# Expert block of a routed layer: the twelve gate and up products in one piece, the next block's token transposes after them

## Chip, cores, metric

One NeuronCore of a Trainium2 chip runs one program. The metric is the device time of one execution in microseconds (us); the median of three runs is given. Engines are named as in the profile: PE is TensorE's matmul, PEld its weight load, DVE is VectorE, ACT is ScalarE, POOL is GpSimd, SP is SyncE. A suffix q (PEldq, DVEq) marks an instruction that the engine's sequencer handles alone, such as register arithmetic, a branch or a wait.

## What is computed

Two transformer-like layers over 2048 tokens of 512 numbers. The first has linear attention and an int8 feed-forward part, the second a gated cumulative attention and a routed part with 32 experts, of which each token uses 8. The change touches only the routed part. Cut to it, the reference is:

```
router_probs = softmax(x @ gate_weight.T); top 8 of 32 experts, some rerouted -> combine[token, expert]
for each expert e:
    gu = x @ wgu[e].T                      # 512 -> 384
    g, u = split(gu, 2)                    # 192 each
    h = silu(g) * u
    y = y + h @ wd[e].T * combine[:, e]    # 192 -> 512
```

## The kernel before

The first 1000 us or so compute the two attention parts, the int8 part and the routing tables. The routed part then works on 159 blocks (NBLK) of 128 rows. A block holds tokens of one expert; on average an expert has five blocks. Each number of the token rows and of h is carried as two float16 numbers, a high half and a low half, and each expert weight too, so a float32 product becomes three float16 products: high by high, high by low, low by high.

What one block k passes through:

- POOL gathers its 128 token rows by an indirect DMA (L1712) into one of eight buffers. It does so eight blocks ahead. Rows of a block are in `xg`, which the trace shows as XT.
- PE transposes them, eight transposes of 128x128 (`gather_transposes`, L816). DVE copies the result out of PSUM in one instruction (L1268) and raises the semaphore `xt_sb`.
- PE computes gate and up together: twelve products of 384 columns (`gate_up`, L825). The list `products` holds the pairs (0,0), (0,1), (1,0) of token half and weight half, four parts of the 512 inputs each. The last one raises `gu_ready`.
- ACT takes silu of the gate half (L1548). DVE multiplies it with the up half and the combine weight (L1278) and raises `h_ready`. ACT writes the high half of h (L1306), DVE the low half in two instructions (L1280, L1281), which raises `h_lo`.
- PE transposes h, three transposes (`h_transposes`, L835). ACT copies them out (L1306), and PE runs five products of 512 columns (`expert_down`, L846) with the down weights.
- ACT scales the result out of PSUM (L1306, X<-bank), and POOL adds it to DRAM by an indirect DMA (L1718). There are two accumulators; a scatter waits for the one two blocks before it.

Each engine has its own instruction stream, written out by hand. PE's iteration for block k is: down products of block k-3, gate and up products of block k with the token transposes of block k+1 in between, h transposes of block k-1. The order on DVE is: copy of the token transposes of block k+1 (it waits for `xt_ready`, L1267 and L1268), h of block k, low half of h of block k. The order on ACT is: silu of block k, copy of the h transposes of block k-1, high half of h of block k, result of block k-2.

The blocks run in a hardware loop unrolled by eight (`every_block`). At the first block of each eight ("fresh") PE and DVE read the packed expert numbers of the next blocks into registers (`load_packs`, L337: one TENSOR_LOAD and some register operations). On PE the loop's branch (L328) and this load stand ahead of the down products of block k-3. The weights of the current expert sit in one of four SBUF slots, so the addresses of the expert's weights are computed by register operations: one (L825, shown by the listing of instructions as ISA) ahead of each of the first eight gate and up products, none ahead of the last four, which reuse the first four's addresses, and four ahead of the five down products.

Waits in PE's iteration: L839 (`ht_sb` of block k-3), L841 (`y_sb`), L859 (weights of the expert), L860 (`xt_sb` of block k; the trace shows it served by the first L825 register operation), L862 (`h_ready`), L811 (the gathered rows of block k+1), L813 (`xt_sb`), L830 (`h_lo` of block k-1), L832 (`ht_sb`).

Of the kernel before, what the change touches and what calls it, by code (L numbers as in the profile page):

```python
# [81 lines left out]
def build(nc, ins, out):  # L82
    ctx = ExitStack()
    with ctx:
# [3 lines left out]
        def sem(name):  # L88
            return ctx.enter_context(nc.semaphore(name))
# [81 lines left out]
        def wc(a, k, c0, n):  # L171
# [107 lines left out]
        xt_ready, xt_sb, gu_ready, sg_ready, h_ready, h_hi, h_lo, ht_ready, ht_sb, blk_done, y_sb = (sem(n) for n in (  # L279
            "xt_ready", "xt_sb", "gu_ready", "sg_ready", "h_ready", "h_hi", "h_lo", "ht_ready", "ht_sb", "blk_done", "y_sb"))  # L280
# [53 lines left out]
        def load_packs(engine, k):  # L334

            at = k.key[0] * 2
            _, words = nc.values_load_multi_w_load_instructions(packs[0:1, bass.ds(at, 3)], (engine,), min_val=0, max_val=(1 << 20) - 1)  # L337
            return words

        def expert_of(words, u):  # L340
            w, shift = words[(u + 4) // 4], (u + 4) % 4
            return (w // (1 << (5 * shift)) if shift else w) % EXPERTS
# [165 lines left out]
        def _(pe):  # L508
# [301 lines left out]
            def gather_transposes(k):  # L810
                pe.wait_ge(xg_in[k.u % NG], k.use(NG) * 16 + 16)  # L811
                if not k.before(2):
                    pe.wait_ge(xt_sb, k.i - 1)  # L813
                d = bank[k.u % 2][:, :].bitcast(F16)
                for c in range(2 * KD):
                    mm = pe.transpose(d[:, c * P:(c + 1) * P], xg[k.u % NG].bitcast(F16)[:, c * P:(c + 1) * P], ident16[:, :])  # L816
                mm.then_inc(xt_ready, 1)

            def weights(sl, j, c0, n):
                return Wslot[:, bass.ds(sl * (2 * WCOLS) + (j * WCOLS + c0), n)]  # L820

            def gate_up(k, sl, some):
                d = bank[2 + k.u % 2][:, 0:2 * DFF]
                for a, b, kd in some:
                    mm = pe.matmul(d, xTb[k.u % 2][:, a * KD + kd, :], weights(sl, b, kd * 2 * DFF, 2 * DFF),  # L825
                                   start=(a, b, kd) == (0, 0, 0), stop=(a, b, kd) == (1, 0, KD - 1))
                return mm

            def h_transposes(k):
                pe.wait_ge(h_lo, k.i + 1)  # L830
                if not k.before(2):
                    pe.wait_ge(ht_sb, k.i - 1)  # L832
                d = bank[4 + k.u % 2][:, :].bitcast(F16)
                for c in range(3):
                    mm = pe.transpose(d[:, c * P:(c + 1) * P], hB[k.u % 2][:, c * P:(c + 1) * P], ident16[:, :])  # L835
                mm.then_inc(ht_ready, 1)

            def expert_down(k, sl):
                pe.wait_ge(ht_sb, k.i + 1)  # L839
                if not k.before(2):  # L840
                    pe.wait_ge(y_sb, k.i - 1)  # L841
                d = bank[6 + k.u % 2][:, :]
                base = KD * 2 * DFF
                order = ((1, 0, base), (1, 1, base), (0, 0, base), (2, 0, base + DIM), (2, 1, base + DIM))
                for n, (c, j, c0) in enumerate(order):
                    mm = pe.matmul(d, hT[k.u % 2][:, c, :], weights(sl, j, c0, DIM), start=n == 0, stop=n == 4)  # L846
                mm.then_inc(blk_done, 1)

            products = [(a, b, kd) for a, b in ((0, 0), (0, 1), (1, 0)) for kd in range(KD)]
            held = {}  # L850

            def expert_block(k, fresh, last=False):
                if fresh:
                    held["packs"] = load_packs(pe.engine, k)
                e = expert_of(held["packs"], k.u)
                if not k.before(3):
                    expert_down(k.at(-3), expert_of(held["packs"], k.u - 3) % NSLOT)
                sl = e % NSLOT
                pe.wait_ge(w_in, e * 16 + 16)  # L859
                pe.wait_ge(xt_sb, k.i + 1)  # L860
                if not k.before(2):
                    pe.wait_ge(h_ready, k.i - 1)  # L862
                gate_up(k, sl, products[:8])
                if not last:
                    gather_transposes(k.at(1))
                gate_up(k, sl, products[8:]).then_inc(gu_ready, 1)
                if not k.before(1):
                    h_transposes(k.at(-1))

            pe.wait_ge(tables_ready, 1)  # L870
            gather_transposes(Blk(0, 0, 8))
            every_block(pe, 8, expert_block, 8)
            final = [Blk(0, NBLK - j, 8) for j in (3, 2, 1)]
            expert_down(final[0], expert_of(held["packs"], NBLK % 8 - 3) % NSLOT)
# [926 lines left out]
```

## Time and profile before

| | us |
|---|---|
| median of 3 runs | 1685.71 |
| lowest, highest | 1683.06, 1691.47 |
| the profiled execution | 1696.52 |
| span in its trace | 1694.7 |
| PE busy in it | 1484.5 (88%) |
| mean granted TensorE clock | 0.945 |

The profiled execution is 10.8 us above the median and 1.8 us longer than its span. Times in the trace are microseconds from the start of the span. A matmul row's own duration includes a modelled end, so how long a group of matmuls holds PE is read from the distance between the starts of groups.

### The profile page before, as it was taken

How to read it: one execution, taken by the hardware profiler on the slowest of the kernel's cores; microseconds unless marked ns; L12 is line 12 of the kernel's file. 1: busy time of each engine (PE TensorE's matmuls, PEld its weight loads, DVE VectorE, ACT ScalarE, POOL GpSimd, SP SyncE). 2: the span in 40 equal slices, each digit the busy share in tenths (PEclk: the TensorE clock that was granted, in tenths of full speed). 3: DMA queues.
4: the chain of work that ended last, by engine and by line, in shares of the span. 5: the costliest groups of instructions: out<-in, count | busy, mean ns of one | idle time of the engine just before them, and what ended most of it. 6: DMA issues, size and time to landing. Idle time of an engine off the chain costs nothing.

```text
span 1694.7 us, 33958 instructions
## 1 busy us (share of the span) xinstructions
PE 1484.5 (88%) x11445; PEld 840.2 (50%) x11446; DVE 974.0 (57%) x1884; ACT 714.9 (42%) x1294; POOL 774.0 (46%) x683
## 2 busy tenths in 40 slices
PE   2699999979999999999996369989988999999980
PEld 1466666644444444445553226545555565665650
DVE  8577777767766666633889664333333343434437
ACT  5233433345454545443555324333433444444430
POOL 3444544451020202044465345565565776666654
PEclk9799999989999999999998569999999999999995
DMA  6331111139786767531111057999999887787868
GB/s 219 113 130 25 25 37 25 25 114 312 258 270 220 264 231 256 183 121 51 52 50 51 3 179 190 249 255 249 263 248 249 161 158 141 143 146 138 147 103 303
DMA packets 96809, 269.44 MB, mean 159 GB/s; under 512 B 15121, under 2 KB 15537, under 8 KB 91889
## 3 DMA queue, kind: packets, MB, share of 16 engines
q1 hardware_dynamic: 61136, 182.75, 32.1%
q0 software_dynamic: 35616, 85.99, 25.9%
q8 instruction: 30, 0.49, 0.1%
q14 instruction: 27, 0.21, 0.0%
HBM read 158.84 MB, written 101.47 MB: 154 GB/s over the span
## 4 chain that ended last, share of the span: by engine, by line
PE 59%; DMA 14%; DVE 14%; issue 6%; ACT 3%; POOL 3%; DVEq 0%; SPq 0%; ACTq 0%; POOLq 0%
PE bank L514 15%; DMA acc<-X,WA 12%; PE bank L825 11%; PE bank L846 6%; PE bank L637 6%; PE bank L643 6%; PE bank L666 6%; PE bank L816 3%; DVE ARENA L1016 2%; ACT ARENA L1306 2%; DMA ARENA<-acc 1%; PE bank L746 1%; DVE ARENA L1194 1%; PE bank L835 1%; PE bank L543 1%
## 5 line engine op out<-in xcount | busy, mean ns | idle before, releaser
L825 PE MATMUL bank<-ARENA,XT 128*128 x1908 | 366.9, 329 | 1.9 <-DVE XT L1268 1.9
L1718 POOL DMA_INDIRECT acc<-X,WA x159 | 252.9, 1590 | 187.1 <-ACT X L1306 143.9
L825 PEld LDWEIGHTS bank<-ARENA,XT 128*128 128x128 f16 x1908 | 181.7, 99 | 125.4 <-issue 10.7
L846 PE MATMUL bank<-ARENA,XT 128*128 x795 | 200.6, 384 | 26.1 <-issue 15.2
L1268 DVE COPY XT<-bank 128x1024 f16<-128x1024 f16 x159 | 109.7, 690 | 189.6 <-PE bank L816 140.3
L1306 ACT ACTIVATE ARENA<-ARENA 128x512 f16<-128x512 f32 (+1 forms) x128 | 92.7, 735 | 263.9 <-DVE ARENA L1044 134.4
L1712 POOL DMA_INDIRECT XT<-x_rows,WA x159 | 157.0, 987 | 56.6 <-issue 35.3
L514 PE MATMUL bank<-WA,XT 128*128 128x512 f16 (+1 forms) x768 | 138.1, 334 | 24.3 <-DVE WA L885 23.5
L1571 POOL TENSOR_TENSOR rstd<-mv,mhalf 128x1 f32<-128x1 f32 x44 | 19.2, 436 | 295.3 <-DVE mv L891 295.3
L514 PE MATMUL bank<-XT,STG 128*128 128x512 f16 x640 | 150.2, 382 | 0.0
L1278 DVE SCALAR_TENSOR_TENSOR XT<-bank,XT 128x192 f32<-128x192 f32 x159 | 66.4, 418 | 140.6 <-ACT XT L1548 117.2
L1548 ACT ACTIVATE XT<-bank 128x192 f32<-128x192 f32 x159 | 52.3, 329 | 212.8 <-PE bank L825 195.1
L1306 ACT ACTIVATE X<-bank 128x512 f32<-128x512 f32 x159 | 93.7, 589 | 114.0 <-DMA acc<-X,WA 86.0
L1306 ACT ACTIVATE XT<-bank 128x384 f16<-128x384 f16 (+2 forms) x207 | 126.0, 609 | 23.9 <-PE bank L503 22.2
L637 PE MATMUL bank<-XT,WA 128*128 (+1 forms) x512 | 122.6, 383 | 8.5 <-issue 8.5
L666 PE MATMUL bank<-ARENA 128*128 128x512 f16 x512 | 121.1, 379 | 3.5 <-DVE ARENA L1050 3.4
L643 PE MATMUL bank<-XT,ARENA 128*128 (+1 forms) x512 | 121.6, 381 | 0.0
L846 PEld LDWEIGHTS bank<-ARENA,XT 128*128 128x128 f16 x795 | 72.8, 98 | 85.8 <-issue 31.0
L1580 POOL TENSOR_TENSOR ARENA<-X,ARENA 128x512 f16<-128x512 f16 (+1 forms) x48 | 68.4, 1436 | 93.1 <-ACT ARENA L1306 93.1
L816 PE MATMUL bank<-ident,XT 128*128 128x128 f16 x1272 | 98.7, 221 | 12.7 <-DMA XT<-x_rows,WA 12.7
L514 PEld LDWEIGHTS bank<-WA,XT 128*128 (+1 forms) x768 | 60.7, 99 | 90.0 <-DVE WA L885 23.1
L816 PEld LDWEIGHTS bank<-ident,XT 128*128 128x128 f16 x1272 | 84.9, 99 | 36.5 <-DMA XT<-x_rows,WA 11.9
(216 smaller groups left out, 2406.7 us busy)
## 6 DMA issues: line engine op xcount, KB each, us to landing
w_scratch<-WA SPq DMA_DIRECT2D x64, 640.0 KB, 3.9
ARENA<-w_scratch SPq DMA_DIRECT2D x32, 1280.0 KB
ARENA<-w_exp SPq DMA_DIRECT2D x48, 640.0 KB, 5.2
WA<-w_exp SPq DMA_DIRECT2D x16, 640.0 KB, 5.0
ARENA<-ARENA SPq DMA_DIRECT2D x64, 128.0 KB, 2.3
acc<-ARENA SPq DMA_DIRECT2D x18, 256.0 KB, 3.0
x_rows<-ARENA SPq DMA_DIRECT2D x17, 256.0 KB, 2.0
STG<-xT SPq DMA_DIRECT2D x8, 512.0 KB, 4.2
```

The source lines that it names most:

```text
L514: mm = pe.matmul(dst, wa(a, k), wb(b, k), start=n == 0, stop=n == 3 * KD - 1)
L637: mm = pe.matmul(bank[0][:, :], Wg[:, n % KD, m * P:(m + 1) * P], XT[:, n // KD, n % KD, tk], start=n == 0, stop=n == 2 * KD - 1)
L643: mm = pe.matmul(bank[1 + m % 2][:, :], Wu[:, n % KD, m * P:(m + 1) * P], XT[:, n // KD, n % KD, tk], start=n == 0, stop=n == 2 * KD - 1)
L666: mm = pe.matmul(bank[4 + tt][:, :], fB[:, m % 2, a, tt * P:(tt + 1) * P], Wd[:, m, :], start=m == 0 and a == 0, stop=m == NM - 1 and a == 1)
L816: mm = pe.transpose(d[:, c * P:(c + 1) * P], xg[k.u % NG].bitcast(F16)[:, c * P:(c + 1) * P], ident16[:, :])
L825: mm = pe.matmul(d, xTb[k.u % 2][:, a * KD + kd, :], weights(sl, b, kd * 2 * DFF, 2 * DFF), start=(a, b, kd) == (0, 0, 0), stop=(a, b, kd) ...
L846: mm = pe.matmul(d, hT[k.u % 2][:, c, :], weights(sl, j, c0, DIM), start=n == 0, stop=n == 4)
L1268: dve.tensor_copy(xTb[k.u % 2].rearrange("p c n -> p (c n)"), bank[k.u % 2][:, :].bitcast(F16)).then_inc(xt_sb, 1)
L1306: return act.activation(dst, src, ACT.Copy, scale=scale)
L1580: pool.tensor_tensor(hl[:, 1, :], tile(t), hl[:, 0, :], ALU.subtract).then_inc(x_lo, 1)
L1712: pool.indirect_dma_start(xg[i % NG], None, xrows, bass.IndirectOffsetOnAxis(blkidx[:, i:i + 1], 0)).then_inc(xg_in[i % NG], 16)
L1718: pool.indirect_dma_start(acc[i % 2], bass.IndirectOffsetOnAxis(blkidx[:, i:i + 1], 0), yD[i % 4], None, compute_op=ALU.add).then_inc(y_ou ...
```

## The change

In PE's iteration the token transposes of block k+1 move from behind the eighth product to behind the twelfth. The signal `gu_ready` stays on the twelfth product. Nothing else moves, and no other engine's order changes.

```
                 if not k.before(2):
                     pe.wait_ge(h_ready, k.i - 1)
-                gate_up(k, sl, products[:8])
+                gate_up(k, sl, products).then_inc(gu_ready, 1)
                 if not last:
                     gather_transposes(k.at(1))
-                gate_up(k, sl, products[8:]).then_inc(gu_ready, 1)
                 if not k.before(1):
                     h_transposes(k.at(-1))
```

On PE, a block in the middle of the unrolled eight. L816 are the token transposes, L825 the gate and up products, L835 the h transposes, and the ISA row of L846 opens the next iteration's down products:

```order
 L825 MATMUL bank3<-ARENA,XT 128x384
 L825 ISA
-L825 MATMUL bank3<-ARENA,XT 128x384
+L825 MATMUL bank3<-ARENA,XT 128x384 x5
 L816 MATMUL bank0<-ident16,XT 128x128 x8
-L825 MATMUL bank3<-ARENA,XT 128x384 x4
 L835 MATMUL bank4<-ident16,XT 128x128 x3
 L846 ISA
```

The four products without register operations now stand behind the eighth one, and eleven transposes follow each other.

On PE, the last block of the unrolled eight, where the loop's branch follows:

```order
 L825 MATMUL bank3<-ARENA,XT 128x384
 L825 ISA
-L825 MATMUL bank3<-ARENA,XT 128x384
+L825 MATMUL bank3<-ARENA,XT 128x384 x5
 L811 ISA
 L816 MATMUL bank0<-ident16,XT 128x128 x8
-L825 MATMUL bank3<-ARENA,XT 128x384 x4
 L835 MATMUL bank4<-ident16,XT 128x128 x3
 L328 REGISTER_ALU
```

The same move; the wait for the gathered rows (L811) moves with the transposes, and the branch still comes right behind the h transposes.

## Rows read from the trace of the kernel before

**Rows 1.** Busy time by stretch of the routed part: us, busy time by engine, PEclk, DMA share.

```profile
core 0: us, PE busy (x) PEld busy (x) DVE busy (x) ACT busy (x) POOL busy (x), PEclk, DMA share, GB/s
1038.00:1095.00 57.00, 54.86 (x422) 34.08 (x420) 22.34 (x58) 23.00 (x58) 31.44 (x25) 1.00 0.89 237
1095.00:1324.00 229.00, 201.78 (x1451) 119.61 (x1449) 78.82 (x211) 84.27 (x209) 135.34 (x105) 0.96 0.93 249
1324.00:1640.00 316.00, 306.84 (x2349) 191.57 (x2348) 128.64 (x334) 133.48 (x335) 217.66 (x169) 1.00 0.81 145
```

**Rows 2.** Timeline, a middle block: start, us, engine line, xcount [idle before it].

```profile
1453.15 0.61 PE L816 MATMUL bank<-ident,XT 128*128 128x128 f16 x8
1453.60 0.81 PE L825 MATMUL bank<-ARENA,XT 128*128 x4
1453.80 0.69 DVE L1268 COPY XT<-bank 128x1024 f16<-128x1024 f16 x1 [1.19 <-issue]
1454.24 0.33 PE L835 MATMUL bank<-ident,XT 128*128 128x128 f16 x3
1454.41 1.24 PE L846 MATMUL bank<-ARENA,XT 128*128 x5
1454.44 0.33 ACT L1548 ACTIVATE XT<-bank 128x192 f32<-128x192 f32 x1 [1.80 <-PE bank L825]
1454.98 0.42 DVE L1278 SCALAR_TENSOR_TENSOR XT<-bank,XT 128x192 f32<-128x192 f32 x1 [0.49 <-ACT XT L1548]
1455.28 1.29 PEld L825 LDWEIGHTS bank<-ARENA,XT 128*128 128x128 f16 x8
1455.49 1.46 PE L825 MATMUL bank<-ARENA,XT 128*128 x8
1456.79 0.61 PE L816 MATMUL bank<-ident,XT 128*128 128x128 f16 x8
```

**Rows 3.** Timeline at the routed part's start, a product that waited for the copy.

```profile
1017.14 0.68 DVE L1268 COPY XT<-bank 128x1024 f16<-128x1024 f16 x1
1018.01 0.42 DVE L1278 SCALAR_TENSOR_TENSOR XT<-bank,XT 128x192 f32<-128x192 f32 x1 [0.19 <-issue]
1018.07 0.23 PEld L825 LDWEIGHTS bank<-ARENA,XT 128*128 128x128 f16 x2 [0.62 <-issue]
1018.07 0.50 PE L825 MATMUL bank<-ARENA,XT 128*128 x2 [0.45 <-DVE XT L1268]
```

**Rows 4.** PE's sequencer around a loop branch, by line (ns, first and last start).

```profile
L825 PEldq FUSED_REGOPS  x8: 46/46/96, 1461.8 to 1462.8; - x8
...
L832 PEldq EVENT_SEMAPHORE  x1: 51/51/51, 1463.2 to 1463.2; - x1
...
L328 PEldq ALU_OP  x1: 32/32/32, 1463.6 to 1463.6; - x1
...
L337 PEldq TENSOR_LOAD <-WA x1: 769/769/769, 1464.1 to 1464.1; - x1
```

**Rows 5.** Timeline from the block before the branch to the second one behind it.

```profile
1461.08 0.69 DVE L1268 COPY XT<-bank 128x1024 f16<-128x1024 f16 x1 [1.13 <-PE bank L816]
...
1462.32 0.42 DVE L1278 SCALAR_TENSOR_TENSOR XT<-bank,XT 128x192 f32<-128x192 f32 x1 [0.55 <-ACT XT L1548]
...
1462.78 1.46 PE L825 MATMUL bank<-ARENA,XT 128*128 x8
...
1463.38 0.22 DVE L1281 TENSOR_TENSOR XT<-XT 128x64 f16<-128x64 f32 x1
...
1466.40 0.77 PEld L846 LDWEIGHTS bank<-ARENA,XT 128*128 128x128 f16 x5 [1.07 <-issue]
1466.43 1.24 PE L846 MATMUL bank<-ARENA,XT 128*128 x5 [0.92 <-ACT XT L1306]
...
1471.15 1.46 PE L825 MATMUL bank<-ARENA,XT 128*128 x8
...
1472.54 0.22 DVE L1281 TENSOR_TENSOR XT<-XT 128x64 f16<-128x64 f32 x1
```

**Rows 6.** Register loads on PE's sequencer, from 1324 us to 1640 us.

```profile
L337 PEldq TENSOR_LOAD <-WA x10: 769/770/1072, 1342.9 to 1615.0; - x10
```

**Rows 7.** Idle time before token transposes and before h transposes, 1040 us to 1324 us.

```profile
  DMA XT<-x_rows,WA: 19.6, 21
...
  DVE XT L1281: 13.9, 24
```

**Rows 8.** Who waited for whom, 1040 us to 1300 us: us, times, longest.

```profile
ACT X L1306 <- DMA acc<-X,WA: 77.7, 21, 6.0
```

More of the change, by code:

```diff
@@ L862, in expert_block @@
                     pe.wait_ge(h_ready, k.i - 1)
-                gate_up(k, sl, products[:8])
+                gate_up(k, sl, products).then_inc(gu_ready, 1)
                 if not last:
                     gather_transposes(k.at(1))
-                gate_up(k, sl, products[8:]).then_inc(gu_ready, 1)
                 if not k.before(1):
```

## The prediction

> **What bounds the kernel now.** I read the busy time by stretch first, since the edit touches only the routed part. From 1324 to 1640 us PE is busy 306.8 of 316 us at full granted clock, so PE sets the pace there, and 84 blocks run. From 1095 to 1324 us PE is busy 201.8 of 229 us, with the DMA engines at 0.93, and blocks come less often. From 1038 to 1095 us PE is busy 54.9 of 57 us [rows 1].
>
> Then the timeline of one middle block. From the start of one group to the start of the next, PE spends 1.30 us on the first eight products (1455.49 to 1456.79), 0.45 on eight token transposes (1453.15 to 1453.60), 0.64 on the last four products, 0.17 on three h transposes and 1.08 on five down products (1454.41 to 1455.49). The sum is 3.64 us, which is also the distance between two blocks (1453.15 to 1456.79): PE never stops in a middle block [rows 2]. There are ten groups of eight in this stretch, since PE's sequencer loads its registers ten times [rows 6]. At such a load PE does stop: the first down product behind it starts at 1466.43, where without a stop it would have started at 1462.78 + 1.30 + 0.45 + 0.64 + 0.17 = 1465.34, by the group lengths above [rows 2, 5]. That is 1.09 us per eight blocks. Check: 84 x 3.64 + 10 x 1.09 = 316.7, the length of the stretch is 316.
>
> Why it stops matters most here. The sequencer rows tell: it takes the first products' register operation at 1461.8, when the DVE copy of the token transposes ends (1461.08 + 0.69 = 1461.77), reaches the waits of the h transposes (L832) at 1463.2 and gets to the loop's branch (L328) at 1463.6, when the low half of h is written (1463.38 + 0.22 = 1463.60). The register load starts at 1464.1 and the first down product's weights at 1466.40 [rows 4, 5]. So branch, load and register work take 2.8 us, and PE is covered only by what the sequencer had queued before it. How early the sequencer gets to the branch is worth PE time, one for one.
>
> **The change part by part.** I use as zero of a block the start of its first product (t0).
>
> *PE's work.* The same 28 matmuls in another order. In each block two changes of kind (product to transpose and back) become one. Eight products take 1.30 us, 0.163 each, four take 0.64, 0.161 each [rows 2], so a change of kind shows no cost to two digits. Term: 0.
>
> *The copy of the token transposes, in middle blocks.* Transposes now start at t0 + 1.30 + 0.64 = 1.94 instead of 1.30. The copy starts 0.65 after them (1453.15 to 1453.80) and takes 0.69 [rows 2], so it ends at t0 + 3.28, and the next block's products are due at 3.64. Before, the copy had 1.00 us to spare, now 0.36. A product that really waited for the copy started 0.25 after its end (1017.14 + 0.68 = 1017.82 to 1018.07), weights and matmul together [rows 3]. So 0.36 - 0.25 = 0.11 us remain and PE does not stop. Term: 0. The weight load of such a first product now starts 0.21 ahead of its matmul (1455.28, 1455.49) [rows 2], and that lead shrinks to 0.11 or less; whether it is needed is a rival below.
>
> *h, in middle blocks.* The copy is ahead of h in DVE's order. Today h waits for silu and starts at 1454.98, which is 3.13 after its block's t0 (1455.49 - 3.64 = 1451.85); now silu comes early (1.94 + 0.20 + 0.33 = 2.47) and h starts behind the copy at 3.28 to 3.47 (the copy of rows 3 was followed by h 0.19 later). So h and its low half are 0.15 to 0.35 later, while the h transposes are due at the same t0 + 2.39 of the next block; the low half ends at 1463.60, 0.82 after t0 [rows 5], so 1.2 us are left. Hidden by the twelve products. Queued behind h on ACT are its high half and the result of block k-2; nobody needs these for another two blocks. SP and POOL are passed by nothing.
>
> *The sequencer at the loop.* Here the cover shrinks. The copy's end, at which the sequencer is let into the next block's products, moves from t0 - 1.01 (1461.77, t0 1462.78) to t0 - 0.36. From there to L832 it took 1.4 us [rows 4], mostly for one register operation per product, which nothing shortens. So it reaches L832 at about t0 + 1.0 and the branch at about t0 + 1.15. Before, it reached the branch at 1463.6, t0 + 0.85, held by the low half of h; that end moves to 0.97 to 1.17, the same place. The branch comes 0.30 us later, the 2.8 us behind it stay, and the down products start 0.30 later. Bounds: 0.1 (only h counts and moves by its least) and 0.64 (the copy's whole delay passes). I take 0.30, as both ways of reckoning agree on it.
>
> *The second block behind the load.* On DVE the register load stands between copy and h, so there h follows the copy at a fixed distance, and the copy is 0.64 later. The low half ended at 1472.54 + 0.22 = 1472.76, t0 + 1.61 of the second block (t0 1471.15) [rows 5]; it will end at 2.25. The h transposes are due at 2.39, so they are just in time, but the sequencer is held until then and must still run the register work of the down products, due at 2.56. One register operation and its product take (1462.8 - 1461.8) / 7 = 0.14 us [rows 4]; the two waits and the first such operation give an estimated 0.3 to 0.4. Term: about 0.07 per eight blocks, bounds 0 and 0.25.
>
> *Sum.* From 1324 us: 10 x (0.30 + 0.07) = 3.7 us. The two groups from 1038 to 1095 us: 0.7 us. The seven others stand where PE idles 27 of 229 us behind the DMA [rows 1]: there a delay is partly made up; half of 2.6 is 1.3 us. Against that stand the late gathers: 21 times PE idled before token transposes, 19.6 us in all [rows 7], and now four more products lie before that wait, up to 0.64 us each. But h transposes waited 24 times for the low half of h, 13.9 us, in the same stretch [rows 7], because ACT had waited for the scatters (77.7 us) [rows 8]; that wait ends when it ends, whatever PE did first. I give the gathers -1 us. Total: 3.7 + 0.7 + 1.3 - 1 = +4.7, say +5 us. Against the profiled execution: 1696.5 + 5 = 1701.5. The three runs' median is 10.8 us lower than that execution, and the terms come from a stretch without DMA noise, so I put the sum on the median: **1690.5 us**, +0.3%. About 0.5% (8.4 us) is what a measurement of this kernel can tell from no change.
>
> **The rivals.**
>
> *Nothing moves (1686).* The sequencer's later arrival is covered after all, or stretch 1095 to 1324 gives back what the groups lose. For: both terms are sums of small delays. Against: the stop at each load is there, ten times.
>
> *Faster (1680).* If the gather waits really shrink and the h transposes behind them are not late, 16 of the 21 waits give 0.6 us: -9.6, with the +4 of the groups left: 1685.7 - 5.6 = 1680. It decides from the point where ACT's waits for scatters no longer follow the late gathers; rows 7 and 8 speak against it.
>
> *Slower (1699).* The lead of the weight load is needed: the first product's weights, possible only 0.11 us before the matmul is due instead of 0.21, hold it up by about that. The place is the first product of each middle block, the price 0.11 x 74 = 8.1 us on top of 5, that is 1698.8. It decides at 0.25 us between copy end and matmul; any further delay (a slower copy, a later semaphore) costs 74 x itself. For: the slack is only 0.11. Against: rows 3, where weights and matmul started together.
>
> *The clock falls (1710).* The granted clock is 1.00 in 316 us with ten stops of 1.1 us each, and 0.96 where PE idles for longer [rows 1]. Should the stop of 1.4 us together with eleven transposes before it bring the lower level, the five down products and eight products behind it take 1.08 + 1.30 more: 10 x 2.4 = 24 us. The Trainium skill (TensorE: Matmul & The Clock Gate, Part 4: PE-mode transpose) says that transposes do not count as PE work for the clock, which speaks against standing eleven in a row. By that rule it would be 1710; by the rows, where eight already stand in a row ahead of products at full clock, nothing.
>
> **How the numbers follow.** The forecast has 0.50, nothing moves 0.20, the gathers' gain 0.10, the weight load 0.14, the clock 0.03, something else 0.03. The range: low end at the gain's 1680, high end 1701, which takes in the weight-load case and the forecast's own upper bound (10 x (0.64 + 0.25) + 2 x 0.89 + 3 = 13.7 us, 1699). Outside are the clock and part of the others. Slower by over 0.5% (above 1694.1): 0.14 + 0.03 + 0.06 of the forecast's upper part and the rest = 0.23. Faster by over 0.5% (below 1677.3): half of the gain's 0.10 and a little of the rest, 0.06. Within 0.5%: 0.71.
>
> **What would show it.** Right: in the new timeline the distance between middle blocks stays 3.64 us; the copy starts 0.65 us behind the first transpose and ends 0.36 before the next product; the branch (L328) comes 1.15 us after t0 and not 0.85; the stop before the down products grows from 1.1 to 1.4 us ten times. Wrong: middle blocks at 3.7 us or more (the weight load), an idle entry of L825 on DVE L1268 in all blocks, a granted clock below 1.00 after 1324 us, or a stop that stays at 1.1 us (nothing moves). If the idle time before token transposes falls far below 19.6 us and that before h transposes does not rise, the gain was real.

## The result: 0.6% slower, and the profile after

| | kernel before | changed kernel |
|---|---|---|
| median, us (10 runs each) | 1690.95 | 1702.5 |
| lowest, highest | 1683.06, 1694.06 | 1694.53, 1707.05 |
| ratio, 95% interval | | 1.0061 (1.0044 to 1.0078) |
| span of the profiled execution | 1694.7 | 1701.1 |

The change costs 0.44 to 0.78%, that is 7 to 13 us, where +5 us were forecast, and its median lies 1.5 us above the top of the range. Part of that is the base: the kernel before has a median of 1690.95 over ten runs, 5.2 us more than the 1685.71 of the first three. Without it the number would have looked right: 1685.71 times 1.0061 is 1696.0, inside the range. The other part, and the one to explain, is that the loss is a little over twice the forecast.

Busy time by stretch in the changed kernel, same columns and nearly the same blocks as [rows 1]:

```profile
core 0: us, PE busy (x) PEld busy (x) DVE busy (x) ACT busy (x) POOL busy (x), PEclk, DMA share, GB/s
1036.80:1094.80 58.00, 55.21 (x422) 34.41 (x421) 21.86 (x60) 24.88 (x59) 33.62 (x26) 1.00 0.89 238
1094.80:1323.60 228.80, 202.84 (x1458) 122.05 (x1457) 77.53 (x208) 85.51 (x209) 134.24 (x104) 0.96 0.92 248
1323.60:1644.40 320.80, 306.69 (x2326) 190.29 (x2325) 120.06 (x332) 140.44 (x333) 216.33 (x168) 1.00 0.78 142
```

PE's busy time in the last stretch is the same (306.7 and 306.8 us), but the stretch is longer. Measured from the same block to the same block, the first token transpose of the 80th to that of the 158th, it is 294.9 us before and 302.6 us after, +7.7 us. From the 9th block to the 80th, which takes in the DMA-bound stretch, it is 301.6 us before and 301.4 after, and the granted clock did not move. The span of this pair of traces differs by 6.4 us in all.

The timeline around one loop branch, to be laid beside [rows 2, 5] (start, us, engine line, count, [idle before it]); DVE and ACT lines have moved up by one:

```profile
1462.20 0.61 PE L816 MATMUL bank<-ident,XT 128*128 128x128 f16 x8
...
1462.85 0.69 DVE L1267 COPY XT<-bank 128x1024 f16<-128x1024 f16 x1 [1.77 <-PE bank L816]
...
1463.46 0.41 DVE L1277 SCALAR_TENSOR_TENSOR XT<-bank,XT 128x192 f32<-128x192 f32 x1
1463.73 1.89 PEld L825 LDWEIGHTS bank<-ARENA,XT 128*128 128x128 f16 x12 [0.16 <-issue]
1463.90 2.11 PE L825 MATMUL bank<-ARENA,XT 128*128 x12
...
1465.85 0.61 PE L816 MATMUL bank<-ident,XT 128*128 128x128 f16 x8
...
1467.77 0.77 PEld L846 LDWEIGHTS bank<-ARENA,XT 128*128 128x128 f16 x5 [1.32 <-issue]
1467.80 1.24 PE L846 MATMUL bank<-ARENA,XT 128*128 x5 [1.17 <-ACT XT L1305]
...
1468.87 2.11 PE L825 MATMUL bank<-ARENA,XT 128*128 x12
...
1471.47 0.69 DVE L1267 COPY XT<-bank 128x1024 f16<-128x1024 f16 x1 [3.10 <-PE bank L816]
...
1472.52 2.11 PE L825 MATMUL bank<-ARENA,XT 128*128 x12
1474.09 0.42 DVE L1277 SCALAR_TENSOR_TENSOR XT<-bank,XT 128x192 f32<-128x192 f32 x1 [1.93 <-issue]
...
1474.47 0.61 PE L816 MATMUL bank<-ident,XT 128*128 128x128 f16 x8
...
1475.14 0.22 DVE L1280 TENSOR_TENSOR XT<-XT 128x64 f16<-128x64 f32 x1
...
1475.42 0.17 PEld L835 LDWEIGHTS bank<-ident,XT 128*128 128x128 f16 x3 [0.52 <-DVE XT L1280]
...
1475.74 1.25 PE L846 MATMUL bank<-ARENA,XT 128*128 x5
```

Three things are to be seen. Middle blocks are still 3.64 us apart (1462.20 to 1465.85). The stop before the first down product behind the branch has grown: the products of that block started at 1463.90 and the down products at 1467.80, 3.90 us later, against 3.65 before (1462.78 to 1466.43). The row of PE names ACT's copy as the end of this wait, but that copy is done at 1467.15; the weight load's row names issue, and the experiments will show that it is the sequencer. And there is a second stop that the kernel before does not have: in the second block behind the branch the h transposes wait 0.5 us for the low half of h, which ends at 1475.36. The down products start at 1475.74, 3.22 after that block's t0 of 1472.52, where 2.56 is due: 0.66 us lost. From token transposes to token transposes the block with the load takes about 4.97 us instead of 4.72 (1465.85 to 1470.82), and the next distance but one, which takes in the second stop, 4.31 instead of 3.64.

PE's sequencer at that branch, as [rows 4]:

```profile
L832 PEldq EVENT_SEMAPHORE  x1: 51/51/51, 1464.9 to 1464.9; - x1
...
L328 PEldq ALU_OP  x1: 32/32/32, 1465.0 to 1465.0; - x1
...
L337 PEldq TENSOR_LOAD <-WA x1: 767/767/767, 1465.5 to 1465.5; - x1
```

It comes to the branch 1.1 us after t0 (the start of the block's first product, 1463.9); before it was 0.85.

The reason for the second stop stands in one row. DVE's register load, in seven groups from 1400 to 1600 us, first before, then after (ns: least, median, most):

```profile
L337 DVEq TENSOR_LOAD <-WA x7: 755/756/756, 1409.1 to 1590.5; - x7
```

```profile
L337 DVEq TENSOR_LOAD <-WA x7: 1314/1337/1367, 1409.4 to 1596.2; - x7
```

The same instruction with the same data takes 0.58 us more. It stands between the copy and h, so h is that much later, on top of the 0.64 that the change had been expected to bring.

### The profile page after: what moved, and what is told of

Same layout as the page of the kernel before. It is cut to its first block, busy times and chain, and to the rows that moved or that the text cites. A ratio compares the mean times of both kernels' runs of the same rounds, so it can differ in the third digit from the quotient of the medians.

```text
span 1701.1 us, 33958 instructions
## 1 busy us (share of the span) xinstructions
PE 1486.6 (87%) x11445; PEld 841.7 (49%) x11446; DVE 963.8 (57%) x1884; ACT 726.1 (43%) x1294; POOL 775.0 (46%) x683
## 4 chain that ended last, share of the span: by engine, by line
PE 58%; DVE 14%; DMA 13%; issue 5%; ACT 4%; POOL 3%; DVEq 1%; SPq 0%; ACTq 0%; POOLq 0%
PE bank L514 14%; DMA acc<-X,WA 12%; PE bank L825 11%; PE bank L846 6%; PE bank L637 6%; PE bank L643 6%; PE bank L666 6%; PE bank L816 3%; DVE ARENA L1015 2%; ACT ARENA L1305 2%; PE bank L746 1%; DVE ARENA L1193 1%; DVEq L337 1%; ACT X L1305 1%; PE bank L835 1%
## 5 line engine op out<-in xcount | busy, mean ns | idle before, releaser
L825 PE MATMUL bank<-ARENA,XT 128*128 x1908 | 342.1, 330 | 2.9 <-DVE XT L1267 2.9
L825 PEld LDWEIGHTS bank<-ARENA,XT 128*128 128x128 f16 x1908 | 188.2, 99 | 148.1 <-issue 33.4
L846 PE MATMUL bank<-ARENA,XT 128*128 x795 | 200.7, 384 | 27.8 <-issue 14.0
L846 PEld LDWEIGHTS bank<-ARENA,XT 128*128 128x128 f16 x795 | 73.3, 98 | 88.1 <-issue 32.8
L816 PE MATMUL bank<-ident,XT 128*128 128x128 f16 x1272 | 98.1, 220 | 8.0 <-DMA XT<-x_rows,WA 7.9
L816 PEld LDWEIGHTS bank<-ident,XT 128*128 128x128 f16 x1272 | 84.8, 99 | 30.1 <-issue 5.5
```

## The experiments

Theory S says that PE's stop at the branch grows one for one with the sequencer's arrival there. Of the slower register load there were three theories. A: a gather's issue slows it (in the changed kernel POOL issues one 0.22 us after the load's start). B: its new place on DVE does it, behind a later copy. C: the first DMA packets of a scatter do (a scatter is POOL's indirect DMA that adds a block's result to DRAM).

**A gather held back.** In the changed kernel, one gather in eight waits:

```
                 if i >= NG:
-                    pool.wait_ge(h_ready, i - NG + 1)
+                    pool.wait_ge(h_ready, i - NG + (3 if i % 8 == 6 else 1))
```

> The changed kernel, but on POOL the gather that used to be issued during the register load of DVE (one gather in eight, the one issued while the first block behind the loop's branch is worked on) waits until that block's h is written. Theory A (the register load on DVE takes 1.34 us instead of 0.76 because a gather is issued within its first 0.25 us): the load comes back to 0.76 us, the second block behind the branch falls from 4.31 to about 3.72 us, ten times after 1323 us and in part of the groups before; 6 to 8 us less than the changed kernel, a ratio of about 1.002 against the kernel before. Rival B (the load is long because it now stands behind a later copy, the gather has no part in it): the load stays at 1.34 us, the second block at 4.31 us, the ratio at 1.006.

Measured: 1703.4 us, ratio 1.0058 (1.0039 to 1.0076). Over seven groups the load is as long as before the edit, and POOL issues nothing in it (load from 1470.8 to 1472.2, POOL's timeline):

```profile
L337 DVEq TENSOR_LOAD <-WA x7: 1341/1348/1396, 1408.5 to 1595.5; - x7
```

```profile
1469.14 1.59 POOL L1717 DMA_INDIRECT acc<-X,WA  x1 [2.01 <-ACT X L1305]
1473.97 0.99 POOL L1711 DMA_INDIRECT XT<-x_rows,WA  x1 [3.25 <-DVE XT L1277]
```

Theory A falls. That leaves the load's place, and the scatter before it, whose issue by POOL ends 0.08 us before the load (1469.14 + 1.59 = 1470.73).

**DVE's load ahead of the copy**, once in the changed kernel and once in the kernel before:

```
+                if fresh:
+                    mine["packs"] = load_packs(dve.engine, k)
                 if not last:
                     xt_evac(k.at(1))
-                if fresh:
-                    mine["packs"] = load_packs(dve.engine, k)
```

> The changed kernel, but DVE does its register load ahead of the copy of the token transposes, in time in which it idled. Theory A and B alike: h of the first block behind the branch no longer waits for the load, so it is written about 2 us earlier, PE's wait for the low half of h in the second block (0.5 us) goes, and that block is back at 3.64 us; the stop before the down products stays at 1.33 us, since PE's sequencer is not touched: 4.95 for the block with the load. Ratio about 1.002. If instead the second block's loss had another cause than a late h (the transposes, the weight load), it stays at 4.31 us and the ratio at 1.006.

Measured: 1696.7 us, ratio 1.0025 (1.0007 to 1.0042), 6 us less than the changed kernel. In the second block behind the branch the down products start 2.57 us after t0 (1470.02 to 1472.59) instead of 3.22, and the block is back at 3.64 us (1470.02 to 1473.66), while the stop at the branch stays (PE's timeline):

```profile
1463.35 0.61 PE L816 MATMUL bank<-ident,XT 128*128 128x128 f16 x8
1463.80 0.33 PE L835 MATMUL bank<-ident,XT 128*128 128x128 f16 x3
1465.30 1.24 PE L846 MATMUL bank<-ARENA,XT 128*128 x5 [1.17 <-ACT XT L1305]
1466.38 2.11 PE L825 MATMUL bank<-ARENA,XT 128*128 x12
...
1470.02 2.11 PE L825 MATMUL bank<-ARENA,XT 128*128 x12
1471.97 0.61 PE L816 MATMUL bank<-ident,XT 128*128 128x128 f16 x8
1472.42 0.33 PE L835 MATMUL bank<-ident,XT 128*128 128x128 f16 x3
1472.59 1.24 PE L846 MATMUL bank<-ARENA,XT 128*128 x5
1473.66 1.63 PE L825 MATMUL bank<-ARENA,XT 128*128 x9
```

So a late h is the whole of the second stop. Ten longer stops at the branch, 2.5 us together, lie within the interval of the loss that is left (0.25%, 0.07 to 0.42).

> The kernel before with the same DVE edit. Theory A: there the late h of the block behind the branch was covered (the h transposes were due 0.7 us after the low half of h), so nothing moves after 1324 us: 4.72 and 3.64 us as before, ratio 1.000. If the load behind the copy had cost something in the kernel before too, at the groups before 1324 us where it took 1.5 us, it is a few us faster, 0.998.

Measured: 1692.7 us, ratio 1.0005 (0.9987 to 1.0024), blocks of 4.73 and 3.64 us as before. In the kernel before, the load was covered.

**The transposes behind the tenth and the eleventh product.**

```
-                gate_up(k, sl, products).then_inc(gu_ready, 1)
+                gate_up(k, sl, products[:10])
                 if not last:
                     gather_transposes(k.at(1))
+                gate_up(k, sl, products[10:]).then_inc(gu_ready, 1)
```

> The transposes stand behind the tenth product, half-way. Theory A: thresholds. The gather is issued 0.5 us after the start of DVE's register load instead of 0.2, and the load takes 0.76 us; the low half of h still decides when the sequencer gets to the branch, so the stop before the down products stays within 0.1 us of 1.09. Ratio 1.000 to 1.002. Rival (both losses grow evenly with the place of the transposes): block with the load 4.84, second block about 3.98, ratio 1.003.

> The transposes stand behind the eleventh product. Theory S: PE's sequencer is let into the products 0.16 us earlier than in the changed kernel and comes to the branch about 0.15 us earlier, so the block with the load takes 4.81 us, between 4.73 (tenth product) and 4.97 (twelfth). Theory C: the scatter's packets start 0.16 us later in DVE's register load than in the changed kernel, at 0.55 us; the load is 0.76 us, or still long if the packets may come that late; with 0.76 the second block takes 3.64 us.

Measured: with ten, 1695.6 us, ratio 1.0011 (0.9996 to 1.0025); with eleven a single run, 1697.0 us. DVE's load, ten first, eleven second:

```profile
L337 DVEq TENSOR_LOAD <-WA x7: 750/752/759, 1408.8 to 1590.2; - x7
```

```profile
L337 DVEq TENSOR_LOAD <-WA x7: 857/860/864, 1408.6 to 1590.8; - x7
```

| transposes behind product | branch, us after t0 | down products, us after t0 | block with the load | DVE's load | second stop |
|---|---|---|---|---|---|
| 8 (before) | 0.96 | 3.65 | 4.72 | 0.76 | 0 |
| 10 | 0.97 | 3.65 | 4.73 | 0.75 | 0 |
| 11 | 1.07 | 3.76 | 4.83 | 0.86 | 0.03 |
| 12 (the change) | 1.22 | 3.90 | 4.97 | 1.34 | 0.66 |

(The branch is here the compare-and-branch instruction, 0.1 us behind the first row of L328; medians of seven groups.) Both losses have a threshold. The low half of h ends 0.82 us after t0 in all four kernels, while the sequencer reaches L832, the wait ahead of the h transposes, at 0.38, 0.69, 0.85 and 1.00. With ten it is still there before the low half of h, and nothing is lost in a steady group; with eleven and twelve the register operations behind the copy decide. From there the branch moves by 0.11 and 0.26 us and the down products by 0.11 and 0.25.

**A later branch in the kernel before**, with no other work:

```
                     h_transposes(k.at(-1))
+                if k.u == 7 and not k.before(8):
+                    for _ in range(4):
+                        pe.wait_ge(h_lo, k.i)
```

> The kernel before, with four more waits on a semaphore long reached in PE's instructions right ahead of the loop's branch; no work is added to any engine, only PE's sequencer comes to the branch later, by about four times 0.1 us. Theory S (the stop before the down products grows one for one with the sequencer's arrival at the branch): the block with the load takes 4.72 + 0.4 = 5.1 us, all others 3.64. Rival (the queue covers such a delay): 4.72.

Measured, a single run: 1698.8 us. The four waits moved the branch by 0.21 us and not by 0.4, to 1.17 after t0. The down products came at 3.87 instead of 3.65 and the block with the load took 4.95 instead of 4.72 us. The size of the dose was wrong by half, but the answer is one for one: theory S stands, and this loss needs neither the new order nor a slower load.

**A scatter held back.** In the changed kernel:

```
                 pool.wait_ge(y_sb, i + 1)
+                if i % 8 == 5 and i + 3 < NBLK:
+                    pool.wait_ge(h_ready, i + 4)
```

> The changed kernel, but on POOL one scatter in eight, the one whose issue ended 0.08 us before DVE's register load began, waits until h of the first block behind the branch is written, so that neither its issue nor the start of its packets lies in that load. Theory C (the load takes 1.34 us because the scatter's packets start 0.4 us into it, after a pause of the DMA engines): the load is back at 0.76 us, the second block behind the branch at about 3.72 us, ratio 1.002 to 1.003 unless the later scatter costs time elsewhere. Theory B (the load is long because of where it stands on DVE, DMA has no part): load 1.34 us, second block 4.31 us, ratio 1.006.

Measured: DVE's load is back at 0.75 us, and the second block at 3.72 us, as theory C said and B did not:

```profile
L337 DVEq TENSOR_LOAD <-WA x7: 750/753/756, 1400.4 to 1587.6; - x7
L337 PEldq TENSOR_LOAD <-WA x6: 1343/1406/1489, 1424.9 to 1580.8; - x6
```

But the kernel is no faster than the changed one: 1704.4 us, ratio 1.0093 (1.0065 to 1.012). The second row says why: now PE's own register load takes 1.41 us instead of 0.77. The first packets of a later scatter run into that one (from 1456.0 us on, the load from 1456.1), and the block with the load takes 5.5 to 5.7 us instead of 4.97. The mechanism has only changed its victim. This second case is less clean than the first, since a gather's issue lies over PE's load too (1455.73 to 1456.72).

The DMA side of it, in slices of 0.4 us. In the changed kernel around the load from 1471.6 to 1472.96 (columns as in the table of stretches above; the last two are DMA share and GB/s; a packet is counted whole in the slice in which it starts, so a share can be above 1), and in the kernel before in its load from 1469.6 to 1470.4:

```profile
1471.60:1472.00 0.40, 0.40 (x4) 0.20 (x2) 0.40 (x1) 0.36 (x1) 0.16 (x1) 1.00 0.00 0
1472.00:1472.40 0.40, 0.40 (x4) 0.15 (x2) 0.16 (x1) 0.13 (x1) 0.40 (x1) 1.00 1.91 82
```

```profile
1469.60:1470.00 0.40, 0.40 (x5) 0.27 (x4) 0.40 (x1) 0.00 (x0) 0.40 (x1) 1.00 0.01 0
1470.00:1470.40 0.40, 0.40 (x6) 0.26 (x4) 0.14 (x1) 0.22 (x1) 0.16 (x1) 1.00 0.00 0
```

In the changed kernel the scatter's first sixteen packets start 0.49 to 0.65 us into the load and are themselves slow: 0.33 to 1.20 us for 2 KB, median 0.75, where later ones take 0.18. They are slow without a load beside them too: 0.34 to 0.74 us in the kernel before, where they start when the load is over. How long DVE's load takes follows the moment at which the first of them starts (packet records of five traces, groups after 1370 us):

| kernel | first scatter packet, us after the load's start | DVE's load, us |
|---|---|---|
| the change, and with the gather held, 16 loads | 0.49 | 1.31 to 1.40 |
| the same two, last load of each | 0.62 | 0.94, 0.97 |
| transposes behind the eleventh product | 0.65 | 0.86 |
| behind the tenth | 0.82 | 0.75 to 0.76 |
| the kernel before | 1.14 | 0.76 |

Traffic as such does not do it. With DVE's load ahead of the copy, 73 to 90 of a scatter's packets were under way during each load, and it took 0.75 to 0.76 us.

**A version that takes stops away.** The kernel before, PE's loop unrolled by sixteen, the register load of the second half (`load_half`, made like `load_packs`) ahead of the h transposes of the eighth block:

```
+                if k.u == 7:
+                    held["packs"] = load_half(pe.engine, k, 1)
                 if not k.before(1):
                     h_transposes(k.at(-1))
...
-            every_block(pe, 8, expert_block, 8)
+            every_block(pe, 16, expert_block, 16)
```

> The kernel before, with PE's loop unrolled by sixteen instead of eight and the register load of its second half put ahead of the h transposes of the eighth block, while products and transposes are still queued. Theory S: that second load is covered by what is queued, so every other stop of 1.09 us falls to between 0 and 0.3 us and the branch is met half as often: about 9 stops fewer, 8 to 10 us faster, ratio 0.995. If the load is not covered there, ratio 1.000.

Measured: 1684.7 us, ratio 0.9961 (0.9944 to 0.9978) against the kernel before, the only version faster than both. The blocks with the load alternate between 4.73 and 3.86 us: where the load stands ahead of the h transposes, what is queued hides all but 0.2 of its 1.09. The gain is 7 us, where 8 to 10 were expected.

The same with the loop unrolled by thirty-two, and three of four loads ahead of the h transposes:

> As the kernel with the second half's register load ahead of the h transposes, but PE's loop unrolled by thirty-two, with three of four loads ahead. Theory S: only four or five blocks still take 4.73 us, the other blocks with a load about 3.85: five more stops of 0.9 us gone, 4 to 5 us faster than the kernel unrolled by sixteen, ratio 0.993 to the kernel before. If the larger loop costs something of its own (its code), it is no faster than that one, 0.996.

Measured: 1693.4 us, ratio 1.0015 (1.0004 to 1.0026): no faster than the kernel before. Its blocks with a covered load take 3.9 us as wished, but at the one branch back to the loop's start in this stretch the compare-and-branch took 4.4 us instead of 0.22. PE worked off what was queued and then stood idle for 5.19 us, and behind that the granted clock was at its lower level (1.2 GHz, 0.50). The branch back before that one, at 1267.9 us, took 6.7 us.

```profile
L328 PEldq COMPARE_BRANCH  x1: 4445/4445/4445, 1396.3 to 1396.3; - x1
```

```profile
1403.21 2.29 PE L851 MATMUL bank<-ARENA,XT 128*128 x5 [5.19 <-issue]
```

```profile
1403.20:1405.50 2.30, 2.29 (x6) 0.94 (x7) 0.00 (x0) 0.00 (x0) 0.00 (x0) 0.50 0.00 0
```

The queues of the pages tell what the larger loop does, that unrolled by sixteen first, by thirty-two second:

```profile
q8 instruction: 37, 0.61, 0.1%
```

```profile
q8 instruction: 73, 1.20, 0.3%
```

The kernel before has 30 such packets, of 16 KB each. Their times tell more: there is none between 1063 and 1620 us in the kernel before, none between 1127 and 1581 with sixteen blocks in the loop, and with thirty-two one follows the other, 3 to 18 us apart, to the end of the routed part. So with thirty-two blocks instructions are fetched in every round. The second case of the expectation holds in kind, but the cost is larger than it said: not 0.996, but 1.0015.

## Why the prediction was wrong

**What bounds the kernel: right.** PE sets the pace after 1324 us, middle blocks stayed at 3.64 us, and all of the loss there lies at the register loads.

**The copy in middle blocks: right.** It ends 0.36 us before the next products (1462.85 + 0.69 = 1463.54, products at 1463.90). The first weight load leads its matmul by 0.17 instead of 0.21 us and costs nothing, so the rival on the weight load falls.

**h in middle blocks: covered, as said, but the size was wrong.** h starts 3.20 after t0 (1463.46, with t0 at 1463.90 - 3.64), where 3.28 to 3.47 was written: it does not even wait for the recorded end of the copy, and was at 3.13 to 3.18 before. Its low half ends 0.82 us after the next t0 (1464.50 + 0.22 = 1464.72), just as before, and not 0.15 to 0.35 later.

**The sequencer at the loop: right in mechanism, slightly too large.** 0.30 us were forecast, 0.25 measured, and the later branch and the splits show it as cause and dose. The sequencer came to L832 at 1.00, as reckoned from the copy. The second way of reckoning, by the low half of h, had 0.97 to 1.17 and is 0.82; that both ways agreed was luck.

**The second block behind the load: the step that failed.** The prediction let the low half of h end 2.25 us after t0 and priced the wait at 0.07 us. It ended at 2.84 (1475.36 - 1472.52), and the wait cost 0.66. The step took the load's duration from the kernel before as fixed, although it moved the load by 0.64 us in time. Where the load stayed short, in the scatter experiment, that block takes 3.72 us, 0.08 more than a middle block: the arithmetic was right, its input was not. The stated bounds, 0 and 0.25, left the duration out too. The trace of before had the warning: between 1030 and 1324 us DVE's nine loads had a median of 1.46 us, and the ten after that 0.76. In the trace eight of the ten groups lose 0.64 to 0.69 us there; the first and the last, with loads of 0.75 and 0.94 us, lose 0.08 and 0.06. That is 5.5 us instead of 0.7, and with 2.2 us at the branch it makes up the 7.7 us measured between the 80th and the 158th block. Put into the sum, the two turn 4.7 into 8.7 us, which lies within the measured 7 to 13.

**The gathers: no gain, as said.** Idle time before token transposes from 1040 to 1324 us fell from 19.6 us in 21 cases to 8.0 in 7, and that before h transposes rose from 13.9 to 20.3:

```profile
  DMA XT<-x_rows,WA: 8.0, 7
...
  DVE XT L1280: 20.3, 27
```

That is [rows 7] again; over half was given back one step later, since ACT still waited for scatters (82.8 us, [rows 8] had 77.7). With the stops at the loads the stretch is as long as before (301.4 and 301.6 us), so the faster rival falls. The single terms of this stretch can't be told apart: it takes from 291 to 302 us in the eleven traces.

**The clock: no.** It stayed at 1.00 after 1323.6 us with eleven transposes in a row. The rule of the Trainium skill (TensorE: Matmul & The Clock Gate, Part 4: PE-mode transpose), that transposes do not count as PE work for the clock, did not show here; nothing in these runs tests it apart from the products around them. The clock rival falls.

**What stays open.** Why a register load is slow when a scatter's first packets start in it was not tried further, nor why these packets are slow. They start about 0.57 us after POOL's issue ends, and nothing here separates the packets from anything else that happens at that moment. It is not the whole rule either. Take as slow a scatter packet of over 0.4 us that starts in a load's first 0.6 us. Over all eleven traces, after 1324 us, none of 182 loads without such a packet took 1 us, and 34 of the other 38 did. Before 1324 us, where the DMA engines are busiest, 60 of 173 loads without one took over 1 us too; 49 of these 60 had a slow packet of another kind in that time. And of the median's +11.5 us (7 to 13 by its interval) the profiled pair shows 7.7 in the last stretch; what lies elsewhere a single pair of traces can't tell.

## What to carry to other kernels

An engine's sequencer is a resource of its own: when a wait releases it later, register work, branches and register loads behind that wait come later, even while the engine's queue still hides the wait. A forecast that moves an instruction in time should ask what it will then run beside, and look through the whole trace for that instruction's longest durations, not only its median in the steady part. And a cover of 0.7 us, 0.64 of which the change itself spends, is none against an instruction whose time varies by 0.6.

## What the runs showed of the hardware

- A register load from SBUF took 0.75 to 0.79 us in most places, also with 73 to 90 packets of a scatter under way, and 1.31 to 1.40 us on DVE when the first packets of a scatter started 0.49 us into it. In the kernel with the scatter held back it took 1.34 to 1.59 us on PE.
- The first sixteen packets of a scatter, 2 KB each, took 0.33 to 1.20 us in the changed kernel at 1472 us and 0.34 to 0.74 in the kernel before, later ones 0.18.
- Four waits on a semaphore long reached cost PE's sequencer 0.21 us together.
- PE's loop of thirty-two blocks (about 2400 PE instructions in the trace) was fetched anew in each round, with 73 packets in the run instead of 30, and two branches back took 6.7 and 4.4 us instead of 0.22. With sixteen blocks (about 1200) there was no such fetch from 1127 us to 1581 us, the rest of the loop.
